# A recommendation tower with a cross network: another order of the first transfers, fewer idle transposes, the last low parts on VectorE, a bias folded into a product

## The reference

```python
for i in range(3):                      # weights W[i]: 128 x (32*G)
    z = (x0[:, :, None, :] * h[:, None, :, :]).reshape(B, F * G, E)
    y = relu(einsum('oc,bce->boe', W[i], z) + b[i][None, :, None])
    x_keep, h = (y[:, :64], y[:, 64:]) if i < 2 else (y, y)
    xs.append(x_keep)
z = concatenate(xs, axis=1).sum(axis=2)                 # 512 x 256
h = maximum(concatenate([z, dense_ctx], 1) @ W_top1 + b_top1, 0)   # 272 -> 512
h = maximum(h @ W_top2 + b_top2, 0)                                # 512 -> 256
y = h @ W_top3                                                     # 256 -> 1
```

## Time and profile before

| | |
|---|---|
| median of three runs | 548.99 us (548.51 to 549.04) |
| profiled execution | 548.4 us, of which 546.6 us are the span from first to last instruction |
| TensorE (PE) busy | 505.7 us, 93% of the span |
| VectorE (DVE) busy | 376.5 us, 69% |
| GpSimd (POOL) busy | 364.1 us, 67% |
| ScalarE (ACT) busy | 198.8 us, 36% |
| mean granted TensorE clock | 0.978 |

### The profile page before, as it was taken

One profiled execution on the slowest core, in us unless ns is written; L12 is line 12 of the kernel. 1 busy time (PEld: TensorE's weight loads), 2 busy tenths in 40 slices (PEclk: granted clock), 3 DMA queues, 4 the chain that ended last, 5 costly groups with the idle time before them and its releaser, 6 DMA issues.

```text
span 546.6 us, 4327 instructions
## 1 busy us (share of the span) xinstructions
PE 505.7 (93%) x1474; PEld 277.4 (51%) x1474; DVE 376.5 (69%) x216; ACT 198.8 (36%) x257; POOL 364.1 (67%) x222
## 2 busy tenths in 40 slices
PE   0977947899999999999999999999999989899988
PEld 0733414455555555565555555555555554455555
DVE  1274526595959595959688695959595968967743
ACT  1212132433444443424342434434443525241244
POOL 5770527497969788796969696969697754715050
PEclk9988887899999999999999999999999999999999
DMA  7697989349997979797878787979789777451200
GB/s 229 144 201 204 210 221 196 100 98 252 222 251 170 255 159 254 158 227 166 230 164 226 172 215 165 225 167 244 164 197 222 171 190 161 90 110 11 74 0 0
DMA packets 33591, 94.49 MB, mean 173 GB/s; under 512 B 7889, under 2 KB 15057, under 8 KB 25122
## 3 DMA queue, kind: packets, MB, share of 16 engines
q1 hardware_dynamic: 27090, 90.82, 69.5%
q10 hardware_dynamic: 2384, 2.35, 2.0%
q0 software_dynamic: 4096, 1.06, 1.6%
HBM read 92.04 MB, written 2.10 MB: 172 GB/s over the span
## 4 chain that ended last, share of the span: by engine, by line
PE 73%; DMA 8%; DVE 7%; issue 4%; POOL 3%; SPq 2%; ACT 1%; POOLq 1%; DVEq 0%; ACTq 0%
PE acc L605 26%; PE acc L618 14%; PE spare L605 12%; PE x_bank L605 11%; DMA x_scratch<-gathered 4%; DVE z L414 4%; PE x_bank L618 3%; PE spare L618 3%; POOL gathered L349 3%; DMA gathered<-in_table,rows_all 2%; DMA x_rot<-x_scratch 1%; SPq L276 1%; POOLq L146 1%; DVE zl_parts L426 1%; PE acc L628 1%
## 5 line engine op out<-in xcount | busy, mean ns | idle before, releaser
L362 POOL TENSOR_TENSOR z_low<-z,z_high 128x1024 fp32r<-128x1024 f32 x90 | 221.4, 2472 | 130.1 <-ACT z_high L498 129.4
L414 DVE TENSOR_TENSOR z<-h,x_pair 128x2048 f32<-128x2048 f32 (+1 forms) x65 | 144.8, 2249 | 106.1 <-ACT h L512 104.6
L605 PE MATMUL acc<-z,w_direct 128*128 128x512 f32 x384 | 176.3, 603 | 15.2 <-DVE z L414 15.2
L349 POOL DMA_INDIRECT gathered<-in_table,rows_all x128 | 142.5, 1113 | 33.4 <-issue 27.1
L498 ACT ACTIVATE z_high<-z 128x1024 fp32r<-128x1024 f32 x90 | 93.3, 1054 | 145.1 <-DVE z L414 124.9
L605 PEld LDWEIGHTS acc<-z,w_direct 128*128 128x128 f32 x384 | 73.6, 193 | 95.7 <-issue 72.6
L605 PE MATMUL spare<-z,w_direct 128*128 128x512 f32 x200 | 92.4, 603 | 4.5 <-DVE z L414 4.5
L605 PE MATMUL x_bank<-z,w_direct 128*128 128x512 f32 x200 | 92.5, 608 | 3.9 <-DVE z L414 3.9
L414 DVE TENSOR_TENSOR z<-h_odd,x_pair 128x2048 f32<-128x2048 f32 x32 | 72.2, 2278 | 8.4 <-ACT h_odd L512 8.4
L414 DVE TENSOR_TENSOR z<-h_even,x_pair 128x2048 f32<-128x2048 f32 x32 | 72.2, 2279 | 7.9 <-ACT h_even L512 7.9
L605 PEld LDWEIGHTS spare<-z,w_direct 128*128 128x128 f32 x200 | 38.4, 193 | 47.9 <-issue 43.0
(11 more groups left out here) (140 smaller groups left out, 266.4 us busy)
## 6 DMA issues: line engine op xcount, KB each, us to landing
x_pair<-x_scratch SPq DMA_DIRECT2D x124, 512.0 KB, 7.3
x_rot<-x_scratch SPq DMA_DIRECT2D x60, 256.0 KB
x_rep<-x_scratch SPq DMA_DIRECT2D x15, 256.0 KB
w_direct<-in_W SPq DMA_DIRECT2D x2, 1024.0 KB, 8.5
gathered<-in_table,rows_all POOLq DMA_INDIRECT x128, 7.1
x_scratch<-gathered SPq DMA_DIRECT2D x32, 64.0 KB, 1.6
x_pair<-x_scratch ACTq DMA_DIRECT2D x4, 512.0 KB, 16.5
x_pair<-in_W_top SPq DMA_DIRECT2D x2, 512.0 KB, 4.7
```

The lines of the kernel that those rows point to most:

```text
L349: pool.indirect_dma_start(gathered[:, c % X_SLOTS, j, :], None, table, bass.IndirectOffsetOnAxis(ap=rows.bitcast(U32), axis=0),).then_inc( ...
L362: nc.gpsimd.tensor_tensor(z_low[:, slot_of(pair)], products_of(pair), z_high[:, slot_of(pair)].bitcast(F32), ALU.subtract).then_inc(low_po ...
L414: nc.vector.tensor_tensor(z[:, step.group % Z_SLOTS, first:end], h[:].unsqueeze(1).to_broadcast([P, end - first, N]), x_pair[:, chunk % 2, ...
L605: op = nc.tensor.matmul(bank_of(pair)[:], w_direct[:, first + i], products_of(pair)[:, i], start=i == 0 and pair is OPENS[pair.layer, pair ...
```

## The change

Six edits, made together:

1. `BUSY` goes from 56 to 28.
2. Transfers at the start: ScalarE's queue issues half pairs only for k = 0 and 1 of chunk 0. On SP the order is now halves (0, k=0 and 1), `store_x(1)`, pairs (0, k=2 and 3) in both halves, `load_x0(1)`, `store_x(2)`, pairs (1, k=0 and 1), then a wait for the products of (0,1,0), `load_x0(2)`, pairs (1, k=2 and 3), and then the loop along `PLAN` from pair (2,0) and `store_x(3)` on.
3. `FIRST` has (2,0,1) before (0,1,0), and TensorE takes the split pairs of (0,1,0) one step later instead of two. The products of (2,0,0), like those of the first step, are made in two halves, with the first half signalled by itself (`HALVED`).
4. The low parts of the two split pairs of (2, 15) are made by VectorE, each behind the products of the next step (`lows`).
5. `b_top1` becomes a 17th row of the dense weights, against a column of ones in the dense inputs (48 rows of three copies become 51).
6. The first dense layer's relu writes its rounded high part at once, VectorE makes the low part as max(bank, 0) minus the high part, and TensorE does the four products that need only the high part before it waits for the low part.

```diff
-BUSY = 56
+BUSY = 28
-FIRST = (... [(2, 0, 0), (0, 1, 0)] + [(2, 0, k) for k in range(1, GROUPS)]
+FIRST = (... [(2, 0, 0), (2, 0, 1), (0, 1, 0), (2, 0, 2), (2, 0, 3)]
 def hands(layer, chunk, k):
-    return tuple("pool" if chunk and (layer, k, i) in AT else "tensor" for i in range(2))
+    low = "vector" if (layer, chunk) == (2, CHUNKS - 1) else "pool"
+    return tuple(low if chunk and (layer, k, i) in AT else "tensor" for i in range(2))
...
-            due[min(n + 2, len(PLAN) - 1)].append(pair)
+            due[min(n + (1 if (pair.layer, pair.chunk) == (0, 1) else 2), len(PLAN) - 1)].append(pair)
...
-            for k in range(GROUPS):
+            for k in range(2):
                 load_half(sp, 0, k, 0)
             store_x(sp, 1)
+            for k in range(2, GROUPS):
+                load_pair(0, k)
             sp.wait_ge(start_done, 1)
             load_x0(sp, 1)
-            for k in range(GROUPS):
+            store_x(sp, 2)
+            for k in range(2):
                 load_pair(1, k)
+            wait_made(sp, STEPS[0, 1, 0])
+            sp.wait_ge(last_made, 2)
+            load_x0(sp, 2)
+            for k in range(2, GROUPS):
+                load_pair(1, k)
...
-                runs = ((0, 2), (2, 4)) if step is PLAN[0] else ((0, 4),)
+                runs = ((0, 2), (2, 4)) if step in HALVED else ((0, 4),)
...
-                for pair in BEHIND[n]:
-                    if pair.by == "vector":
-                        low_part(pair)
+                for pair in LOWS[n]:          # due at n + 1
+                    low_part(pair)
...
+                nc.vector.scalar_tensor_tensor(out=hid1_low[:, m, :], in0=top_bank[m][:], scalar=0.0,
+                                               in1=hid1_high[:, m, :].bitcast(F32), op0=ALU.max,
+                                               op1=ALU.subtract).then_inc(hid1_ready, 1)
...
-                nc.scalar.activation(hid1[:, m, :], top_bank[m][:], ACT.Relu,
-                                     bias=bt1[:, m:m + 1]).then_inc(hid1_made, 1)
-                act.wait_ge(hid1_made, m + 1)
-                nc.scalar.activation(hid1_high[:, m, :], hid1[:, m, :], ACT.Copy).then_inc(hid1_rounded, 1)
+                nc.scalar.activation(hid1_high[:, m, :], top_bank[m][:], ACT.Relu).then_inc(hid1_rounded, 1)
...
             for k in range(4):
+                pe.wait_ge(hid1_rounded, k + 1)
+                for m in range(2):
+                    cols = slice(k * 2 * P + m * P, k * 2 * P + (m + 1) * P)
+                    nc.tensor.matmul(acc[m][:], wt2_high[:, cols], hid1_high[:, k, :], start=k == 0, stop=False)
+                    nc.tensor.matmul(acc[m][:], wt2_low[:, cols], hid1_high[:, k, :], start=False, stop=False)
                 pe.wait_ge(hid1_ready, k + 1)
```

More of the change, by code:

```diff
@@ L66 @@
 OF = {0: 1, 1: 0, 2: -1}
-FIRST = ([(1, 0, k) for k in range(GROUPS)] + [(2, 0, 0), (0, 1, 0)] + [(2, 0, k) for k in range(1, GROUPS)]
+FIRST = ([(1, 0, k) for k in range(GROUPS)] + [(2, 0, 0), (2, 0, 1), (0, 1, 0), (2, 0, 2), (2, 0, 3)]
          + [(1, 1, 0), (0, 2, 0)] + [(1, 1, k) for k in range(1, GROUPS)])
@@ L122, in behind, with lows @@
         for pair in step.by("vector", "pool"):
-            due[min(n + 2, len(PLAN) - 1)].append(pair)
+            due[min(n + (1 if (pair.layer, pair.chunk) == (0, 1) else 2), len(PLAN) - 1)].append(pair)
     return due
-BEHIND = behind()
+def lows():
+    due = {n: [] for n in range(len(PLAN))}
+    for n, step in enumerate(PLAN):
+        for pair in step.by("vector"):
+            due[min(n + 1, len(PLAN) - 1)].append(pair)
+    return due
+BEHIND, LOWS = behind(), lows()
+HALVED = (STEPS[1, 0, 0], STEPS[2, 0, 0])
 ORDER = list(START.pairs)
@@ L142, in flat, with dlrm_tower @@
     return tiles.rearrange("p t o -> p (t o)")
-def dlrm_tower(nc, idx_in, row0_in, ident_in, sel_in, signs_in, columns_in, table, dense, w0_in, w12_in, w_top1, w_top2, out):
+def dlrm_tower(nc, idx_in, row0_in, ident_in, sel_in, signs_in, columns_in, table, dense, w0_in, w12_in, w_dense, w_top1, w_top2, out):
     with ExitStack() as ctx:
@@ L211, in dlrm_tower @@
         wt2 = flat(x_pair[:, 0, 8:10, :])
-        wd = x_pair[0:COPIES * EMBED, 0, 10, :]
+        wd = x_pair[0:COPIES * DENSE, 0, 10, :]
         wt1_high, wt1_low = z_high[:, PAIR_SLOTS - 1], z_low[:, PAIR_SLOTS - 1]
@@ L334, in _ @@
             wait_made(sp, STEPS[2, CHUNKS - 2, GROUPS - 1])
-            tops = [(wd[EMBED * i:EMBED * (i + 1)], w_top1[2 * P:, :]) for i in range(COPIES)] + [
-                (wt1, w_top1[0:2 * P, :].rearrange("(k p) n -> p k n", p=P)),
+            tops = [(wd[DENSE * i:DENSE * (i + 1)], w_dense) for i in range(COPIES)] + [
+                (wt1, w_top1.rearrange("(k p) n -> p k n", p=P)),
                 (wt2.rearrange("p (k n) -> p k n", k=4), w_top2.rearrange("(k p) n -> p k n", p=P))]
@@ L543, in _ @@
             act.wait_ge(dense_turned, 1)
-            nc.scalar.activation(dense_high[:], dense_bank[0:COPIES * EMBED, :], ACT.Copy).then_inc(dense_rounded, 1)
+            nc.scalar.activation(dense_high[:], dense_bank[0:COPIES * DENSE, :], ACT.Copy).then_inc(dense_rounded, 1)
             act.wait_ge(x_stored[0], 32)
-            for k in range(GROUPS):
+            for k in range(2):
                 load_half(act, 0, k, 1)
@@ L598, in unsplit @@
                     pe.wait_ge(w12_here[pair.layer - 1], 16)
-                if step is PLAN[0] and pair.i == 0:
-                    pe.wait_ge(first_made, 1)
+                if step in HALVED and pair.i == 0:
+                    pe.wait_ge(first_made, HALVED.index(step) + 1)
                 else:
@@ L679, in _ @@
             for k in range(4):
+                pe.wait_ge(hid1_rounded, k + 1)
[3 more added lines that the diff above has]
+                    nc.tensor.matmul(acc[m][:], wt2_low[:, cols], hid1_high[:, k, :], start=False, stop=False)
                 pe.wait_ge(hid1_ready, k + 1)
                 for m in range(2):
-                    first = k * 2 * P + m * P
-                    op = three_products(acc[m], (wt2_high, wt2_low), slice(first, first + P),
-                                        (hid1_high[:, k, :], hid1_low[:, k, :]), k == 0, k == 3)
+                    cols = slice(k * 2 * P + m * P, k * 2 * P + (m + 1) * P)
+                    op = nc.tensor.matmul(acc[m][:], wt2_high[:, cols], hid1_low[:, k, :], start=False, stop=k == 3)
                     if k == 3:
@@ L710 @@
     signs[2::GROUP, 1] = -1.0
-    signs[2 * EMBED:COPIES * EMBED, 2] = -1.0
-    signs[1 * EMBED:2 * EMBED, 3] = -1.0
+    signs[2 * DENSE:COPIES * DENSE, 2] = -1.0
+    signs[1 * DENSE:2 * DENSE, 3] = -1.0
     arrays = {
@@ L719 @@
         "table": np.concatenate(tables, axis=0),
-        "dense_ctx": np.asarray(inputs["dense_ctx"]),
+        "dense": np.concatenate([np.asarray(inputs["dense_ctx"]), np.ones((BATCH, 1), np.float32)], axis=1),
     }
@@ L734 @@
         arrays[f"W{i}"] = w.transpose(1, 3, 2, 0).reshape(P, -1)
-    for name in ("W_top1", "W_top2"):
-        arrays[name] = np.asarray(inputs[name])
-    per_row = [inputs[name] for name in ("L0_rec_b0", "L0_rec_b1", "L0_rec_b2", "b_top1", "b_top2", "W_top3")]
+    w_top1 = np.asarray(inputs["W_top1"])
+    arrays["W_dense"] = np.concatenate([w_top1[2 * P:], np.asarray(inputs["b_top1"])[None]], axis=0)
+    arrays["W_top1"], arrays["W_top2"] = w_top1[0:2 * P], np.asarray(inputs["W_top2"])
+    per_row = [inputs[name] for name in ("L0_rec_b0", "L0_rec_b1", "L0_rec_b2", "b_top2", "W_top3")]
     arrays["columns"] = np.concatenate([np.asarray(a).reshape(-1, P) for a in per_row], axis=0).T
```

37 lines of the change are left out of this document (18 added, 19 removed).

## The result

The changed kernel takes 544.42 us (median of four runs, 542.92 to 546.40) against 548.75 for the kernel before; the ratio is 0.9942, with a 95% interval of 0.9916 to 0.9968. It is faster, by 4.3 us of the medians, where 7.85 were forecast. The time lies inside the range of 538 to 546, but outside the forecast's own 539.5 to 543. The ratio's 0.58% is 3.2 us, 40% of the forecast. The profiled execution is the longest of the four, 546.4 us with a span of 544.6, so its trace shows only 2 us of the gain. What follows compares stamps with this in mind.

The account below looks back on a forecast made before the run. TensorE, 93% busy, was taken to bound the kernel, its 11 us wait before (1,1,1) being a late transfer. -8.4 (wait) +0.8 (clock) -0.25 (end) = -7.85 us, from 548.99 to 541.1; forecast 539.5 to 543 (0.50), range 538 to 546 (0.80).

Parts of the forecast that it names:

- Transposes: Start: with 28 the last ends at 18.8 instead of 21.89 us; the 3.0 us gained are swallowed by chunk 0's loads.
- rival (e): Start: with half the transposes the clock's rise does not come or is lost in the spread matmuls; 543.5 us, chance 0.07.
- Chunk 0's pairs: SP's loads at the start: k = 2 lands at 38.1, k = 3 at 42.7 us; with the transposes +0.15 us.
- Rival (b): Start: chunk 1's gathers land as late as before, at 34.8, so k = 3 at 46.5; 545 us, chance 0.16.
- The swap: (2,0,1) before (0,1,0): the latter's product ends at 56.0 instead of 54.7, low parts by 63, TensorE at 64.6; costs nothing.
- The long wait: Before (1,1,1): load_x0(2) lands in time, TensorE starts at 77.4 instead of 85.79, -8.4 us, still idling from 73.9.
- The clock: TensorE after the 3.5 us wait before (1,1,1): a lowered clock costs 0 to +1.4 us more, taken as +0.8.
- The end: Last products and dense layers: +0.1 for a 2.0 us wait before (2,15,3), -0.37 for an earlier dense start; together -0.25.
- (a): Start: loads less binding, (1,0,3) ends near 47 and the clock falls less; 537 to 539 us, chance 0.14.
- (c): The reorder buys nothing: load_x0(2) lands at 77, (1,1,1) starts at 82.5+2; 548 to 549.5 us, chance 0.06.
- (d): Slower: SP stands at store_x(1) for chunk 1's gathers, chunk 0's last two pairs behind it; 551 us, chance 0.05.
- (f): End: 17-row dense weight transfers run on one engine, 7.3 us instead of 1.8 each; chance of an effect 0.02.

Follow-up runs that it names:

- x2_busy56: The changed kernel with 56 idle transposes again (BUSY = 56): 544.98 us, 0.9944 against the kernel before.
- x1_pairs_early: The changed kernel with chunk 0's four pairs all issued first again, in halves from both queues, ahead of store_x(1): 539.35 us, 0.9842 against the kernel before.
- x8_early_and_k3: x1_pairs_early with the first bank's three products ahead of the second's at k = 3 of the last dense products: 538.36 us, 0.9822 against the kernel before.
- x10_early_busy56: x8_early_and_k3 with 56 idle transposes (BUSY = 56): 541.80 us, 0.9862 against the kernel before.
- x6_gathers_held: The changed kernel with GpSimd waiting for chunk 0's pairs before it gathers chunk 2: 551.79 us, 1.0068 against the kernel before.
- x7_no_swap: The changed kernel with (0,1,0) again ahead of (2,0,1) and its split pairs two steps behind: 547.37 us, 0.9982 against the kernel before.
- x11_early_no_swap: x8_early_and_k3 with (0,1,0) again ahead of (2,0,1) and its split pairs two steps behind: 539.85 us, 0.9852 against the kernel before.
- x5_sp_order_only: The kernel before with only the new SP order from load_x0(1) on, chunk 0's pairs as before: 541.14 us, 0.9878 against the kernel before.
- x9_chunk1_order: x8_early_and_k3 with (1,1,1) ahead of (0,2,0), whose split pairs come one step behind instead of two: 538.37 us, 0.9813 against the kernel before.
- x4_store2_early: The kernel before with only store_x(2) moved ahead of chunk 1's pairs on SP: 546.48 us, 0.9975 against the kernel before.

## Why the prediction was wrong

The sign and the main mechanism were right. The size was off, by 3.5 us of the medians (4.7 by the ratio), and one term alone is 4.6 us.

*Transposes.* Right. The last of 28 ended at 18.8, as worked out (18.8 to 19.5 in the other traces with 28). The slow first ones are seen again: 11 in the two microseconds from 14 us and 21 in those from 18 us in x2_busy56, though the clock column shows 1.00 in both. But of the 3.05 us won at the first spread product, only 1.35 are left at (1,0,0), 31.72 instead of 33.07: the clock was 0.50 from 24 to 26 us in this trace, and eight records of the start took 5.40 us instead of 3.70. That is rival (e) in part; x1_pairs_early and x8_early_and_k3 show no such fall. What is left is hidden, as forecast (x2_busy56); what the transposes are worth with the pairs early is not settled (x10_early_busy56).

*Chunk 0's pairs* is the step that failed: "k = 2 lands at 31.9+1.6+4.6 = 38.1, k = 3 at 42.7". They came at 42.1 and 47.4, so (2,0,0) started at 56.3 instead of 51.7. It is k = 3 that TensorE waits for. Of its 4.7 us, 1.15 are the issue (33.05 instead of 31.9), some 2 are the gathers of chunk 2 beside it, which the sum left out (x6_gathers_held), and 1.4 are left without them; for k = 2 these are 1.15, 1.1 to 1.7 and 1.2.

The sum counted the pairs' own bytes as if they went alone: 2.1 MB at 0.23 per us. The trace has SP's queue moving 3.21 MB between the issue of these pairs and the landing of k = 3 (1.83 until k = 2, for 1.05), at 92.8% of the engines' time. Behind them on SP stood `load_x0(1)`, 1.3 MB issued from 35.5 on, and from 42.4 on the store of chunk 2 and its followers; so about a megabyte of what stood behind went in first. In x6_gathers_held it is 2.55 MB, so part of this excess is there without the gathers, and more with them. The gathers themselves take 5.4% of the engines' time, 0.8 us of the 14.4, for 0.07 MB; how they cost 2 us is not shown. Nor did any run hold `load_x0(1)` until the pairs had landed, which would test whether it costs the 1.4. Rival (b) named the late gathers and gave 545, near the result, but blamed the end of chunk 1's gathers (32.2, not 34.8), not the ones beside the pairs: that its number is near is luck.

*Halved products.* Right: the wait is 2.83 instead of 3.89, 1.06 us.

*The swap* "costs nothing" was wrong twice. TensorE idles 1.79 us before (2,0,2): it did the two steps before in 7.1 us at the full clock, and the product for (2,0,2), which my sum did not follow, was made only then, behind that of (0,1,0). Where those steps ran partly at the low clock, after the same wait of 2.83 (8.59 us, x8_early_and_k3), only 0.30 was left. And without the swap it is not the same: 1.2 us longer up to (1,1,1) in the traces of both x7_no_swap and x11_early_no_swap, and 2.2 and 1.6 us slower by the ratios, both at the edge of what the intervals tell.

*The long wait.* `load_x0(2)` was in time, and the store of chunk 2 early; x5_sp_order_only gives 6.7 us by itself, against -8.4 less 1.07 and plus the clock's 0.8, -6.5 by the sum; with an interval of 4.7 to 8.7 and a wait left that was mis-sized, so close a match is partly luck. The wait left was forecast at 3.5 and is 5.18: the term mis-sized is `zl_parts`, 2.65 us instead of 0.74. The trace of the kernel before had this length twice already, ahead of its two late idle moments:

```profile
434.36 2.86 DVE L426 SCALAR_TENSOR_TENSOR zl_parts<-zl_high,signs,zl_full 128x512 fp32r<-128x512 f32 x1
```

GpSimd's low part of (1,1,0) starts at 76.83, while VectorE's product runs till 77.86, and is itself stretched to 3.24 us from some 2.4; `zl_parts`, started at 77.97, ends 0.55 us after it. The Trainium skill ("Trainium Architecture — The Big Picture", "What this means for kernel authors") says that VectorE and GpSimd share a port pair that one of them locks; these lengths agree. x9_chunk1_order takes (0,2,0) out of this place, but the collision moves with it (3.57 us).

*The clock.* +0.8 was taken for (1,1,1); by the trace it is 1.2: from 82.88 to 88.88 for what took 85.79 to 90.60 before. The step at 104.11 ran at the full clock in this trace (3.70 us) and not in others (5.40, x1_pairs_early and x8_early_and_k3), after the same wait of 2.14.

*The end.* "Together -0.25" came out as nothing. The wait of 1.55 did become one elsewhere, of 1.75 where 2.0 was drawn up. The 0.37 us of an earlier start are lost at k = 3, where the new order closes the two banks 0.23 us apart instead of 0.68, so that ScalarE's last relu starts 0.45 later (x8_early_and_k3). I had counted 24 products as 24 and not looked at which comes last.

*Rivals.* (a) describes x1_pairs_early, not the change. (c), (d) and (f) did not come: `x0` of chunk 2 was in time, and the 17-row transfers were done before 512 us. Chunk 3's `x0` was no wait either.

By parts, then: SP's order from `load_x0(1)` on, -6.7; the halves, swap, transposes and end together another 2.0 (x1_pairs_early has 0.9842 against 0.9878 for x5_sp_order_only, and the intervals overlap; no run has the halves alone); holding back half of chunk 0's pairs, +5.5. The best kernels measured here are x8_early_and_k3 and x9_chunk1_order, 0.9822 and 0.9813, 6 to 7 us faster than the changed one.

## What to carry to other kernels

Before moving a transfer behind a wait, ask what the chip does in that time: here two pairs that VectorE was ready for by 35 us stood behind a gather until 32 us, while the transfer that was really late could be had by reordering the queue behind it (x5_sp_order_only). Count all that the queue and the engines carry until a transfer lands, not its own bytes alone: here it was 3.2 MB for pairs of 2.1. And where an edit reorders products of several banks, look at which bank closes last and who waits for it.

## What the runs showed of the hardware

The granted clock fell in some executions while TensorE was never idle. With 56 transposes and the same instructions for TensorE, x2_busy56 kept 1.00 and x10_early_busy56 did not. Stretches of the two, the last three columns being clock, DMA share and GB/s:

```profile
24.00:28.00 4.00, 4.00 (x10) 1.57 (x9) 3.56 (x7) 2.04 (x6) 3.09 (x4) 1.00 1.01 231
28.00:32.00 4.00, 2.13 (x6) 0.76 (x4) 1.41 (x4) 1.79 (x3) 3.08 (x4) 1.00 0.49 99
```

```profile
24.00:28.00 4.00, 4.00 (x7) 1.18 (x5) 2.06 (x3) 2.67 (x7) 3.08 (x4) 0.69 1.04 233
28.00:32.00 4.00, 4.00 (x6) 1.82 (x6) 2.69 (x6) 0.00 (x0) 3.06 (x4) 0.50 1.01 225
```

In both, TensorE did the spread products, which use 32 of the rows, and then the start's. (1,0,0) comes at 36.95 instead of 32.96, 4 us later; 0.65 of that was there before the fall, at the end of the transposes. The two differ in chunk 0's loads, but the fall comes and goes without such a difference: the kernel before and x5_sp_order_only do the same up to there, loads included, and have 1.00 and 0.71 from 24 to 28, and x8_early_and_k3 and x9_chunk1_order have 1.00 and 0.57. The fall was seen in the trace of x4_store2_early too (0.66), and for some 2 us in that of the changed kernel (0.59). What brings it about, no run shows. Runs of one kernel differ too: x5_sp_order_only took 540.8 to 541.3 four times and 544.7 and 545.3 twice, its profiled run being the 544.7. That these two groups are the two kinds of start is likely, but only the profiled runs show their clock. It also means that a median of four, like that of the change, carries an uncertainty of its own of a microsecond or more, and that the 4.3 us are not a sharp number.
